# Eight indirect DMAs at a time: GpSimd waits for each group of eight scatters and of eight gathers

## The reference

```python
x = x + tanh(g_xattn[0]) * L0_xattn(layernorm(x), ctx)      # fp8-style quantised product with ctx
x = x + tanh(g_ffn[0])   * L0_ffn(layernorm(x), w1, w2)      # ternary weights, gelu twice
x = x + tanh(g_xattn[1]) * L1_xattn(layernorm(x), ctx, ctx, mask, Wq, Wk, Wv, Wo)   # 16 heads
x = x + tanh(g_ffn[1])   * L1_ffn(layernorm(x), router, experts, shared)
# L1_ffn: softmax over 8 router logits, the best 2 of 8 experts for each token, renormalised;
#   moe = sum over the 2 chosen of share * (silu(x @ gate_e) * (x @ up_e)) @ down_e     (512 -> 352 -> 512)
#   out = moe + (silu(x @ s_gate + b) * (x @ s_up + b)) @ s_down + b                     (512 -> 704 -> 512)
```

## Time and profile before

| | us |
|---|---|
| median of three runs | 1144.55 |
| the three runs | 1143.68, 1144.55, 1148.33 |
| span of the profiled execution (first to last instruction) | 1146.9 |
| own time of the profiled execution | not on the page; its span is all that is told |
| PE busy | 1028.8 (90% of the span) |
| POOL busy | 456.0 (40%) |
| scatters issued, first to last | 809.1 to 851.3 |
| second block begins | 859.5 |
| gathers issued, first to last | 1093.7 to 1136.6 |

### The profile page before, as it was taken

How to read it: one execution, slowest core, us unless ns; L and a number is a source line. 1 busy time by engine, 2 the same in 40 slices (tenths; PEclk the granted TensorE clock), 3 DMA queues, 4 the chain that set the end, 5 groups by cost and what they waited for, 6 DMA issues and landing times. The chain is left out here.

```text
span 1146.9 us, 17729 instructions
## 1 busy us (share of the span) xinstructions
PE 1028.8 (90%) x5438; PEld 475.5 (41%) x5439; DVE 747.0 (65%) x1419; ACT 601.8 (52%) x898; POOL 456.0 (40%) x483
## 2 busy tenths in 40 slices
PE   0466889999789999999999998999998899999996
PEld 0243445555423223323322324455445455555542
DVE  6988988888786776578477547745545344443347
ACT  6897999999346776467467565452211111111110
POOL 1100335544410242243134341000657788889065
PEclk9978899999979999999999999998999899999998
DMA  9322930000534234134211004201678888976588
GB/s 325 114 74 80 342 138 1 2 1 9 133 89 107 80 82 116 62 58 94 66 48 44 12 21 136 76 26 52 243 282 170 200 205 207 206 192 146 153 284 291
DMA packets 174204, 142.39 MB, mean 124 GB/s; under 512 B 121364, under 2 KB 137108, under 8 KB 173624
## 3 DMA queue, kind: packets, MB, share of 16 engines
q1 hardware_dynamic: 163560, 110.40, 34.7%
q0 software_dynamic: 8672, 29.76, 7.9%
q10 hardware_dynamic: 1904, 1.38, 0.6%
HBM read 70.93 MB, written 43.37 MB: 100 GB/s over the span
## 5 line engine op out<-in xcount | busy, mean ns | idle before, releaser
L1432 ACT ACTIVATE prob<-p_col,mask_col,any_key 128x512 f32<-128x512 f32 x256 | 186.2, 781 | 103.2 <-PE p_col L1564 102.3
L1653 DVE CUSTOM_DVE_ANT_0 ajunk<-p_row,mask_row 128x512 bf16<-128x512 f32 x256 | 166.2, 686 | 64.1 <-PE p_row L1513 62.5
L1526 PE MATMUL p_out<-prob,v 128*64 128x512 f32 x512 | 138.1, 618 | 0.1
L1332 POOL TENSOR_TENSOR o<-sum_a,rec 32x512 f32<-32x512 f32 x30 | 39.1, 1304 | 186.1 <-DMA rec<-inv_d 184.0
L1513 PE MATMUL p_row<-ks,early_place 99*128 99x512 f16 x256 | 100.5, 395 | 8.7 <-DVE top L1653 8.0
L1564 PE MATMUL p_col<-early_place,ks 101*128 101x512 f16 x256 | 97.7, 385 | 0.9 <-ACT prob L1432 0.3
L2647 DVE SCALAR_TENSOR_TENSOR shid<-s_up,ssilu 128x352 f32<-128x352 f32 x39 | 20.4, 524 | 99.0 <-PE s_up L2565 98.8
L2513 ACT ACTIVATE ssilu<-s_gate 128x352 f32<-128x352 f32 x39 | 18.1, 463 | 124.0 <-PE s_gate L2565 124.0
L2578 PE MATMUL s_down<-mw,shT 128*128 (+1 forms) x351 | 82.0, 379 | 0.0
L2565 PE MATMUL s_gate<-mw,sxT 128*128 x444 | 74.1, 318 | 6.7 <-DMA sxT<-x_slots 6.7
L2565 PE MATMUL s_up<-mw,sxT 128*128 x444 | 73.5, 316 | 0.0
(11 more groups left out here) (354 smaller groups left out, 2077.3 us busy)
## 6 DMA issues: line engine op xcount, KB each, us to landing
x_slots<-nought SPq DMA_DIRECT2D x3, 3328.0 KB, 18.4
y_slots<-y SPq DMA_DIRECT2D x39, 256.0 KB, 2.2
early_place<-in_ctx SPq DMA_DIRECT2D x8, 1024.0 KB, 6.2
early_place<-halves_d SPq DMA_DIRECT2D x45, 128.0 KB, 2.5
halves_d<-halves SPq DMA_DIRECT2D x18, 256.0 KB, 2.1
mstg<-in_L_ffn_gate_w POOLq DMA_DIRECT2D x6, 704.0 KB, 5.7
mstg<-in_L_ffn_up_w POOLq DMA_DIRECT2D x6, 704.0 KB, 6.0
x<-in_x SPq DMA_DIRECT2D x4, 1024.0 KB, 7.3
```

Of the source, the lines that this page charges most:

```text
L1432: nc.scalar.activation(prob[s % 4][:, c, :], p_col[c][:], ACT.Exp, bias=mask_col[:, b, k:k + 1], scale=any_key[:, b:b + 1]).then_inc(t_exp, 1)
L1526: mm = nc.tensor.matmul(p_out[pr][c * 2 * DH:(c + 1) * 2 * DH, :], v1[b % 2][:, k, g, :], prob[n % 4][:, c, :], start=(k == 0), stop=(k == ...
L1653: nc.vector.tensor_tensor_reduce(junk[:, n % 2, :], p_row[n % 2][:], mask_row[:, blk // HPG, :], 1.0, -3e38, ALU.add, ALU.max, top[blk % 2 ...
```

## The change

Two waits are added to POOL's lists, each in a loop over the 16 token tiles. Before the scatters of tiles 4, 8 and 12 POOL waits until the eight, sixteen and twenty-four scatters already issued have landed. Before the gathers of tiles 4, 8 and 12 it waits until the eight gathers of the batch before have landed. These are six waits in all; no instruction is added, removed or moved, and the counts for which the other engines wait are as they were.

```diff
             pool.wait_ge(m_dest, 1)
             for t in range(NT):
+                if t and t % TPB == 0:
+                    pool.wait_ge(m_scat, 16 * 2 * t)
                 for s in range(2):
                     nc.gpsimd.indirect_dma_start(out=x_slots, out_offset=bass.IndirectOffsetOnAxis(ap=dest[:, s, t:t + 1], axis=0),
                                                  in_=row_of(t), in_offset=None).then_inc(m_scat, 16)
...
             pool.wait_ge(e_stored[1], 16 * PAIRS_OF_TILES)
             for t in range(NT):
+                if t and t % TPB == 0:
+                    pool.wait_ge(e_gathered[t // TPB - 1], 16 * 2 * TPB)
                 for s in range(2):
                     nc.gpsimd.indirect_dma_start(out=gathered[:, t, s, :], out_offset=None, in_=y_slots,
```

## The result

The changed kernel takes 1168.0 us in the median of four runs (1162.9 to 1172.7), against 1146.4 for the kernel before in the same sessions: a ratio of 1.0173 with a 95% interval of 1.013 to 1.0216. It is slower, by about what was forecast. The profiled execution took 1166.0 us, with a span of 1164.2.

What follows compares the result with a forecast made beforehand. From the first gather on, POOL's issues were taken to bound the end; scatter delays counted beyond 2.3 us. Gathers 12.0, scatters 9.4 and PE 1.2 made 22.6 us on 1144.55: 1167 us, range 1154 to 1178.

Steps and rivals of the forecast that it cites:

- room: End of the first block: SP waits 2.3 us for PE, so a scatter phase later by that much delays nothing.
- long issue: Gathers: one issue by POOL takes 3.17 us among issues of 0.94 to 0.95; the forecast kept it.
- first scatter wait: Before the ninth scatter: the eighth lands 9.6 us after issue, beside SP's stores; cost 8.0 us, the largest term.
- the later two: Second and third scatter waits: landings of 3.0 us as in the last group, 1.84 us each.
- the short landings: Rival, 1150 us, chance 0.08: with eight in flight, each DMA waited for takes the shortest time seen; 5.8 us in all.
- the stores: Rival, 1190 us, chance 0.05: SP's stores, stretched by the waits, meet all scatter groups, likewise the stores of `x`.
- first gather wait: Before the ninth gather: the eighth lands 7.4 us after issue; cost 6.2 us.
- The second and third: Later gather waits: landings at the medians of their groups, 4.8 and 4.5 us; cost 3.45 and 3.2 us.
- The last landing: End of the gathers: the last gather's landing falls from 6.27 to 5.5 us, giving back 0.8 us.
- PE's slower first products: Start of the second block: after a longer idle time PE's first products take 3.70 + 2.94 us, adding 1.2 us.
- The rival of the late start: Second block, 1160 us, chance 0.10: starting later puts a transposing load beside less traffic, giving back 7.3 us.

Runs made afterwards that it cites:

- scat_last: control with only the third scatter wait, before the 25th scatter for all 24 before it; one run, first scatter to second block 52.5 us.
- both_again: control with all six waits; ratio 1.0209 to the kernel before.
- gath_only: control with only the three waits at the gathers; ratio 1.0117 to the kernel before.
- stores_later: control with the scatter waits, SP's stores to shared_d and late_d held until the first eight scatters landed; one run, first two waits 2.04 and 9.13 us.
- scat_only: control with only the three waits at the scatters; ratio 1.0092 to the kernel before.
- control: The kernel before, with PE's wait for an expert's weights written as a wait against at least 1; ratio 1.0006 to the kernel before.
- gath_two_back: control with POOL waiting, at the gathers of tiles 8 and 12, for the group before the last one; ratio 1.0002 to the kernel before.

## Why the prediction was right

Two sums hold for all twelve traces, to within 0.6 us for the first and 0.7 for the second. The scatter phase is 50.4 us, plus the waits at scatters, less a room of some 2.3 us: 60.4 for the changed kernel (60.1 measured), 52.8 for scat_last (52.5), 59.7 for both_again (59.2). The gather phase is 51.2 us, plus the waits at gathers, plus 2.2 where there is a long issue: 65.9 for the changed kernel (65.8), 64.8 for gath_only (65.2), 67.2 for both_again (66.9).

By the prediction's steps: the first scatter wait was put at 8.0 us and cost 7.9; the later two at 1.84 each, and cost 2.7 and 1.7, since the 16th scatter took 3.7 us to land and not 3.0. The cause given for the first, SP's stores, is shown by stores_later. The scatters were to delay the second block by 9.4 us, and did by 9.6. Two of the rivals fell with these rows: of the short landings, 2.7 us at each scatter, only the third wait met one, and the stores did not run beside every group.

The first gather wait was put at 6.2 and cost 6.2, with some luck: the landing was 7.2 us and not 7.4, and POOL went on 0.26 us after it and not 0.1, the figure taken from SP. The second and third were put at 3.45 and 3.2, and cost 4.3 and 4.1: the eighth gather of a group lands 5.1 to 5.3 us after its issue (the chain has 1124.04 to 1129.35 for the second), where I had taken the median of a group.

These same gathers, the 16th and the 24th, took only 3.5 and 3.7 us in the kernel before. The premise that the stores of finished `x` pieces fall beside them as before did not hold. The first of these stores, SP's timeline before and after:

```profile
1116.76 18.55 SPq L2446 DMA_DIRECT2D out_x<-x  x3
...
1121.68 28.47 SPq L2448 DMA_DIRECT2D out_x<-x  x3
```

Before, the 16th gather (1115.08) went out 1.7 us ahead of the first store; now (1124.04) it goes out 2.4 us behind it, while the store is in flight. In the twelve traces the 16th and 24th gathers took 4.3 to 5.3 us in the six cases in which such a store was in flight at their issue, and 3.5 to 4.2 in the other 18. No run moved the stores, so that they are the cause is argued from this and not shown.

The last landing was to give back 0.8 us. The 32nd gather did land sooner, in 5.2 us instead of 6.27, but nothing came back: from its issue to the end of the span it is 10.2 us against 10.3, since the chain now goes through the 30th gather, which takes 6.46, and DVE. Against these errors stands the long issue, 2.2 us, which I had kept and which this kernel does not have. So that the gathers' 12.0 us came out as 12.6 in the profile is in part luck.

PE's slower first products were to cost 1.2 us. They took 3.70 + 2.24 instead of 3.26 + 2.17, 0.5 us.

The rival of the late start, with its chance of 0.10, is what the one profile of the changed kernel seems to show, 4.9 us given back. Over all executions it is not borne out: the middle stretch is 229.3 to 233.4 us in the five kernels with a scatter wait and 231.1 to 238.8 in the seven without. A mean difference of some 2 us is within that spread, and the times of scat_only and both_again leave little room for it. In that stretch of the traces PE is idle for 3.5 us in the changed kernel and for up to 10.8 in the control, which waits 4.35 and 4.95 us for two transposing loads; in seven kernels PE waits for POOL's weight work too, and its busy time runs from 223.8 to 228.0 us. Why these waits fall differently from execution to execution stays open.

## What to carry to other kernels

A wait for the newest of a row of transfers costs the time to landing, and here some 0.26 us until POOL goes on, less the issue interval, once for each wait, where the issuing engine is on the path. A wait for the group before the last one cost nothing that could be measured here, and still bounds what is in flight, at two groups instead of one. Before such a wait is priced, look at what else the DMA engines move beside the group in question: it made 1.7 us and 7.9 us out of the same wait. A landing time read from the kernel without waits holds only while the waits do not push the transfer beside other traffic. And one profile of a stretch that varies by several us between executions can show a gain that is not there.

## What was not expected of the hardware

One indirect DMA among the 32 gathers took POOL 3.16 to 3.32 us to issue instead of 0.95, in the same place in five kernels, in another place in a sixth, and nowhere in the other six. It was absent with waits that never bit (gath_two_back) and with one wait far ahead of it (scat_last), and present with three such waits (scat_only). Each kernel was traced once, so whether the program or the execution decides is not shown. What it is was not found; it takes 2.2 us more of POOL's time than a usual issue.
